# A decoder's feed-forward stage: roundings on Scalar, output rows added by Vector, centring and weighting on GpSimd, down product two batches behind

## What is computed

```python
def rms_norm(x, g):
    var = jnp.mean(x * x, axis=-1, keepdims=True)
    return x * jax.lax.rsqrt(var + EPS) * g
def activation_quant(x):
    scale = 127.0 / jnp.clip(jnp.max(jnp.abs(x), axis=-1, keepdims=True), 1e-05, None)
    return jnp.clip(jnp.round(x * scale), -128, 127) / scale
def bit_linear(x, w, g):
    xn = rms_norm(x, g)
    xq = ste(xn, activation_quant(xn))
    wq = ste(w, weight_quant(w))
    return xq @ wq.T
y = bit_linear(x, gate_w, gate_norm_w)          # 512 -> 2 x 1408
gate, up = jnp.split(y, 2, axis=-1)
h = gate * jax.nn.sigmoid(gate) * up
return bit_linear(h, down_w, down_norm_w)       # 1408 -> 512
# x = x + _L0_ffn_ref(_layernorm(x, axis=-1), ...)
```

## Time and profile before

| | |
|---|---|
| three timed runs | 1201.27, 1203.71, 1204.38 us; median 1203.71 |
| the profiled execution | 1201.6 us, its span 1199.8 us |
| busy share of the span | PE 86%, DVE 68%, ACT 54%, POOL 54% |
| feed-forward stage | from 996.2 us to the end of the span |
| one batch in its loop | 11.42 us |
| mean granted clock of PE over the span | 0.948 |

### The profile page before, as it was taken

One profiled execution on the slowest core, in us unless ns is written; L12 is line 12 of the kernel. 1 busy time (PEld: TensorE's weight loads), 2 busy tenths in 40 slices (PEclk: granted clock), 3 DMA queues, 4 the chain that ended last, 5 costly groups with the idle time before them and its releaser, 6 DMA issues. The chain is left out here.

```text
span 1199.8 us, 25407 instructions
## 1 busy us (share of the span) xinstructions
PE 1026.7 (86%) x9588; PEld 773.0 (64%) x9604; DVE 812.5 (68%) x1487; ACT 652.1 (54%) x1188; POOL 644.6 (54%) x584
## 2 busy tenths in 40 slices
PE   5689999999999999999754899999999944777675
PEld 5568887888888888888542566666666621433332
DVE  7687776666666666667532777778777636888884
ACT  5554555445454544546532476767776522555553
POOL 3663766656565665656635235445453335566663
PEclk9799999999999999999885999999999966899998
DMA  9042634323332332334536687878867010000000
GB/s 346 31 176 106 259 123 161 141 75 137 141 124 89 141 140 74 138 141 170 194 111 142 158 175 174 193 176 187 180 146 157 21 28 24 18 26 17 26 27 27
DMA packets 51135, 147.57 MB, mean 123 GB/s; under 512 B 10448, under 2 KB 24272, under 8 KB 39760
## 3 DMA queue, kind: packets, MB, share of 16 engines
q1 hardware_dynamic: 42288, 86.93, 27.3%
q0 software_dynamic: 8064, 58.72, 13.4%
q10 hardware_dynamic: 672, 0.40, 0.1%
HBM read 120.46 MB, written 25.17 MB: 121 GB/s over the span
## 5 line engine op out<-in xcount | busy, mean ns | idle before, releaser
L1291 DVE TENSOR_REDUCE mx<-Sm 128x4 f32<-128x768 f32 x128 | 122.6, 958 | 83.7 <-PE Sm L1032 81.5
L282 PE MATMUL Qb<-a_xTh,WqH 128*128 128x256 f32 x512 | 147.0, 287 | 3.3 <-DVE a_vl L800 3.2
L283 PE MATMUL Qb<-a_xTl,WqH 128*128 128x256 f32 x512 | 146.3, 286 | 0.0
L284 PE MATMUL Qb<-a_xTh,WqL 128*128 128x256 f32 x512 | 146.1, 285 | 0.0
L627 POOL TENSOR_TENSOR a_pr<-a_pr_plain,a_ph 128x512 fp32r<-128x512 f32 x64 | 83.7, 1308 | 110.9 <-ACT a_ph L447 110.8
L740 DVE TENSOR_TENSOR a_turned<-Qb,sinS 64x512 f32<-64x512 f32 (+1 forms) x144 | 94.9, 659 | 62.5 <-PE Qb L284 45.0
L609 POOL TENSOR_TENSOR a_ql<-a_rot,a_qh 128x512 fp32r<-128x512 f32 x64 | 84.1, 1318 | 98.2 <-ACT a_qh L467 98.0
L1130 ACT ACTIVATE x_ex<-Se 128x768 f32<-128x768 f32 x128 | 103.8, 811 | 60.1 <-PE Se L1032 60.0
L459 ACT ACTIVATE Lb<-Lb 128x512 f32<-128x512 f32 x64 | 37.2, 582 | 171.0 <-PE Ob L354 170.9
L367 PE MATMUL Yb<-a_WoH,a_oH 128*128 128x512 f32 x256 | 104.8, 409 | 4.3 <-POOL a_oN L605 4.3
L282 PEld LDWEIGHTS Qb<-a_xTh,WqH 128*128 128x128 f32 x512 | 99.4, 194 | 7.1 <-issue 2.6
(11 more groups left out here) (202 smaller groups left out, 2840.3 us busy)
## 6 DMA issues: line engine op xcount, KB each, us to landing
a_WoH<-wo_parts POOLq DMA_DIRECT2D x28, 1024.0 KB, 5.2
a_WoL<-wo_parts POOLq DMA_DIRECT2D x28, 1024.0 KB, 7.1
K<-k_parts SPq DMA_DIRECT2D x32, 256.0 KB, 7.7
q_parts<-x_qp SPq DMA_DIRECT2D x16, 384.0 KB, 3.0
k_parts<-x_kp SPq DMA_DIRECT2D x16, 384.0 KB, 3.4
Q<-q_parts SPq DMA_DIRECT2D x16, 384.0 KB, 5.3
a_w_stage<-in_gateT SPq DMA_DIRECT2D x8, 704.0 KB, 4.1
x_w_stage<-in_gateT SPq DMA_DIRECT2D x8, 704.0 KB, 5.2
```

What stands on the lines that cost most here:

```text
L282: pe.matmul(out, w_hi(k), xTh[:, k, :], start=(k == 0), stop=False)
L283: pe.matmul(out, w_hi(k), xTl[:, k, :], start=False, stop=False)
L284: mm = pe.matmul(out, w_lo(k), xTh[:, k, :], start=False, stop=(k == KD - 1))
L1291: dve.tensor_reduce(mx[:, half, at:at + 4].rearrange("p (j a) -> p j a", j=2), Sm[:, :, 0:2 * WIN].rearrange("p j (a c) -> p j a c", a=2), ...
```

## The change

The feed-forward stage is written anew, on the same tiles and chunks:

- The rounding multiplications `xr` and `hr` move from Vector to Scalar (an activation Copy with a scale pointer and MAGIC as bias). Vector keeps `xq` and `hq`.
- `xn` is gone: GpSimd subtracts the row's mean (`xc`) and multiplies by `g1` (`xg`). The row's `scale` is multiplied into `bound` and `ascale` by Vector instead.
- `f1` and `f2` are formed by GpSimd, as two-tensor operations on one column. `f1` has four columns, `hg` two buffers.
- `ys` and GpSimd's add are gone: Vector adds the output rows straight from `Yf`, in one operation `added` that writes `X`.
- The squares are scaled when taken, and the sum of three is formed by `hsum` (of two, early) and `hms`.
- PE's `down` is that of b-2 and stands between gate and up of chunk 0 and chunk 1; the hidden transpose of b-1 stands last in the step. The scale and the rounding of the hidden rows of b-1 come in step b, behind the first `h` of b.
- Every step is written out (b from -3 to 17), with no loop; each small result has a semaphore of its own.

The core of the diff, by queue:

```diff
-            dve.tensor_scalar(t["wf"][:, :], w_mean[:, :], 1.0 / 127.0, None, ALU.mult)
+            for i, factor in ((0, 1.0 / 127.0), (1, 127.0 ** -2)):
+                dve.tensor_scalar(t["wf"][:, i:i + 1], w_mean[:, i:i + 1], factor, None, ALU.mult)
...
+        def steps(step):
+            for b in range(-3, B + 2):
+                step(b)
...
         @block.tensor
             def step(b):
                 if real(b):
-                    pe.wait_ge(xqT_ready, done(b, 1, 0))
-                    for c in range(NC):
-                        gate_up(b, par, c)
+                    gate_up(b, 0)
+                if real(b - 2):
+                    down(b - 2)
+                if real(b):
+                    gate_up(b, 1)
+                if real(b + 1):
+                    rows_turned(b + 1)
+                if real(b):
+                    gate_up(b, 2)
                 if real(b - 1):
+                    hidden_turned(b - 1)
...
         @block.scalar
+            def rows_rounded(b):
+                wait(act, ascale_ready, b + 1)
+                wait(act, xq_ready, b)
+                act.activation(xr[:, :], xg[:, :], ACT.Copy, bias=MAGIC, scale=ascale[:, 0:1]).then_inc(xr_ready, 1)
+            def hidden_rounded(b):
+                wait(act, hscale_ready, b + 1)
+                wait(act, hq_ready, b)
+                act.activation(hr[:, :], hg[b % 2][:, :], ACT.Copy, bias=MAGIC, scale=hscale[:, 0:1]).then_inc(hr_ready, 1)
-                    act.activation(ys[:, :], Yb[:, :], ACT.Copy, scale=f2[:, 1 - par:2 - par]).then_inc(ys_ready, 1)
...
         @block.gpsimd
+                if real(b):
+                    weighted(b, 0)
+                if real(b - 1):
+                    wait(pool, hbound_ready, b)
+                    wait(pool, x_done, b - 2)
+                    pool.tensor_tensor(f2[:, (b - 1) % 2:(b - 1) % 2 + 1], hbound[:, :], t["wf"][:, 1:2], ALU.mult).then_inc(f2_ready, 1)
+                if real(b + 3):
+                    wait(pool, xr_ready, b + 3)
+                    pool.tensor_scalar(xc[:, :], t["X"][:, b + 3, :], t["mv"][:, b + 3, 0:1], None, ALU.subtract).then_inc(xc_ready, 1)
+                    wait(pool, xc_ready, b + 4)
+                    pool.tensor_tensor(xg[:, :], xc[:, :], t["g1"][:, :], ALU.mult).then_inc(xg_ready, 1)
+                if real(b + 2):
+                    wait(pool, bound_ready, b + 3)
+                    wait(pool, h_ready, NC * (b - 1))
+                    pool.tensor_tensor(f1[:, (b + 2) % 4:(b + 2) % 4 + 1], bound[:, :], t["wf"][:, 0:1], ALU.mult).then_inc(f1_ready, 1)
+                if real(b):
+                    weighted(b, 1)
+                    weighted(b, 2)
+                    wait(pool, hms_ready, b + 1)
+                    wait(pool, hscale_ready, b)
                     pool.tensor_tensor(rms[:, :], hms[:, :], t["half"][:, :], ALU.pow).then_inc(rms_ready, 1)
-                    pool.tensor_tensor(x, x, ys[:, :], ALU.add).then_inc(x_done, 1)
...
         @block.vector
+            def added(b):
+                wait(dve, y_full, b + 1)
+                wait(dve, f2_ready, b + 1)
+                dve.scalar_tensor_tensor(out=t["X"][:, b, :], in0=Yb[:, :], scalar=f2[:, b % 2:b % 2 + 1], in1=t["X"][:, b, :],
+                                         op0=ALU.mult, op1=ALU.add).then_inc(x_done, 1)
+            def step(b):
+                if real(b - 1):
+                    hidden_maximum(b - 1, 2)
+                    mean_square(b - 1)
+                if real(b):
+                    hidden(b, 0)
+                if real(b - 1):
+                    hidden_scale(b - 1)
+                if real(b + 2):
+                    rows_scale(b + 2)
+                if real(b - 2):
+                    added(b - 2)
+                if real(b - 1):
+                    hidden_quantised(b - 1)
+                if real(b):
+                    hidden_maximum(b, 0)
+                    hidden(b, 1)
+                if real(b + 2):
+                    rows_quantised(b + 2)
+                if real(b):
+                    hidden_maximum(b, 1)
+                    hidden(b, 2)
+                    first_squares(b)
```

More of the change, by code:

```diff
@@ L1405, in ffn @@
 def ffn(nc, t, out):
-    H0 = 2
     with ExitStack() as ctx:
@@ L1437, in ffn @@
[L1437 to L1440, removed]
+        h, hr = sb("h", [P, F], F32), sb("hr", [P, F], F32)
+        hg = [sb(f"hg{i}", [P, F], F32) for i in range(2)]
+        sq, ss = sb("sq", [P, 512], F32), sb("ss", [P, NC], F32)
+        hq, hqT = sb("hq", [P, F], BF16), sb("hqT", [P, F], BF16)
@@ L1453, in ffn, with wait @@
         block = ctx.enter_context(nc.Block())
[L1455 to L1468, removed]
+        def wait(eng, signal, count):
+            if count > 0:
+                eng.wait_ge(signal, count)
@@ new lines, in down @@
+            def down(b):
+                wait(pe, hqT_ready, b + 1)
+                wait(pe, x_done, b)
+                for k in range(KF):
+                    mm = pe.matmul(Yb[:, :], hqT[:, k * P:(k + 1) * P], t["downQ"][:, k * D:(k + 1) * D],
+                                   start=(k == 0), stop=(k == KF - 1))
+                mm.then_inc(y_full, 1)
+            def step(b):
+                if real(b):
+                    gate_up(b, 0)
[7 more added lines that the diff above has]
+                    gate_up(b, 2)
+                if real(b - 1):
+                    hidden_turned(b - 1)
@@ L1518, in _ @@
+            steps(step)
         @block.scalar
@@ L1531, in squares @@
             def squares(b, c):
                 lo, hi = CHUNKS[c]
[L1533 to L1542 removed]
+                wait(act, h_ready, NC * b + c + 1)
@@ L1595, in _ @@
+            steps(step)
         @block.sync
         def _(sp):
-            with sp.Fori(0, B) as b:
-                sp.wait_ge(x_done, b + 1)
-                sp.dma_start(out[bass.ds(b, 1), :, :].rearrange("a t d -> t (a d)"),
-                             t["X"][:, bass.ds(b, 1), :].rearrange("p a d -> p (a d)")).then_inc(out_done, 16)
-            sp.wait_ge(out_done, 16 * B)
+            for b in range(B):
+                wait(sp, x_done, b + 1)
+                sp.dma_start(out[b], t["X"][:, b, :]).then_inc(out_done, 16)
@@ L1603, in _ @@
+            wait(sp, out_done, 16 * B)
         @block.vector
         def _(dve):
[L1605 to L1615 removed]
```

298 lines of the change are left out of this document (117 added, 181 removed).

## The result

| | median | runs | ratio to before, 95% interval |
|---|---|---|---|
| before | 1202.60 us | 9 | |
| changed | 1207.99 us (1203.02 to 1209.53) | 9 | 1.0036 [1.0019, 1.0052] |

The forecast was 1198.9 with a range up to 1207.5; the median lies 0.5 us above its end and 9.1 above the forecast. The profiled execution of the changed kernel took 1203.0 us, the fastest of its nine; that of before took 1201.6.

A forecast was written before the change was run, and what follows sets the result against it. Vector was taken to be full before, a ring of waits to bound the changed kernel at 11.05 us a batch; +4.1 - 4.1 - 5.6 + 0.8 = -4.8 us gave 1198.9 on the timed runs' scale, range 1193 to 1207.5.

The forecast's parts named there:

- The ring: Feed-forward loop: a closed chain of waits through Vector, Scalar and GpSimd sets the batch period, 11.05 us instead of 11.42.
- (b): Scalar, after the batch's first `h`: `hr`, a square and `xr`, done 4.33 us after that `h` starts.
- step (d): GpSimd: `xq`, asked for during `xg`, takes its turn, then `f1` and `hg` of chunk 1, done at 8.14 us.
- term (c): GpSimd, behind `xr`: `xc` 0.90 us, `xg` 1.27 and two handovers of 0.07, done at 6.63 us.
- Rival 2: GpSimd's `xc` dearer than any two-tensor operation, through its pointer; slower by over 0.3% from 1.55 us; chance 0.12.
- the rule of 1.5 us for each 0.1: Whole kernel: up to 1.1 us, every 0.1 us on `xc` adds 1.5 us to the total.
- The sum's terms: Feed-forward stage: start +4.1, first two batches -4.1, batch 2 to 15 -5.6, end +0.8 us; together -4.8.
- The clock: PE: longest early pause 1.8 us, granted clock 1.0 from about 15 us on, last `down` at the low clock.
- 1 (`xc` at 1.27): GpSimd's new operations cost what its others do: period 11.47 us, total 1205.0, no change that can be told; chance 0.17.
- 3 (no ring, 1181): The chain of waits doesn't close; Scalar's and Vector's chain of some 9.9 us limits a batch, total 1181; chance 0.03.
- 4, on sharing: Vector's `xq` takes its turn ahead of GpSimd's `xg`, up to 0.3 us a batch, +3.9, total 1202.8; chance 0.13.
- `xqT` in the start: Start of the feed-forward stage: Scalar's first `xqT` comes at 9.0 us, behind the second batch's `xr`; before, 4.86.

The follow-up runs named there:

- e1: Changed kernel with GpSimd's `hg` of chunk 1 moved between `xc` and `xg`, ahead of `xg` and `f1`: 1186.98 us, ratio to before 0.9865.
- e2: Changed kernel with the centring `xc` moved from GpSimd to Vector, behind `hq`: 1187.39 us, ratio to before 0.9867.
- e3: Changed kernel without the centring `xc`, so its result is not the same: 1184.36 us, ratio to before 0.9843.
- e4: Changed kernel with the mean given to `xc` as a broadcast second tensor instead of a pointer: 1198.9 us, ratio to before 0.997.
- second profile: The changed kernel, unaltered, timed and profiled once more: 1208.12 us, ratio to before 1.0043; its profiled execution took 1208.1 us.

## Why the prediction was wrong, point by point

**What bounded before, and what the change frees.** Right. `hq` is 0.88 without GpSimd beside it (0.89 forecast), Vector's work fell to 84.2/126 of 11.55, 7.7 us (7.4 forecast), `hr` is 1.47 (1.45) and `xr` 0.71 (0.72). Two sums of work were off without consequence, since neither engine is full: Scalar has 7.3 us a batch (7.9 forecast), PE 9.0 (8.3).

**The ring.** Right in its order, and e1, e2, e3 and e4 each changed the period as the ring has it: 10.20, 10.44, 10.09 and 11.13, where 10.2, 10.5, 10.1 and 11.35 were written with the measured `xc` at hand. Counted from `h` at 1079.31: `xc` starts at 4.33 (forecast for the end of (b): 4.33), the maximum of chunk 1 at 8.69 instead of 8.14, the next `h` at 11.55 instead of 11.05. The whole difference arises between `xc` and that maximum: +0.67 for `xc`, -0.13 as `xq` no longer takes its turn ahead of `f1`. The waits on Vector stand where they were forecast: 1.0 ahead of the maximum of chunk 2, and 2.5 instead of 1.4 ahead of that of chunk 1. Half of this 1.1 is the late maximum (0.55); the other half is a link of step (d) that didn't occur: `xq` was to be held by `xg` and take 1.2, but `xc` was still running when it was asked for, and it took 0.67.

**The step that failed: term (c), `xc` at 0.90.** It is 1.57 in the loop and 1.60 in the mean:

```profile
L1570 POOL TENSOR_TENSOR f_hg<-f_h,g 128x512 f32<-128x512 f32 x32 | 40.7, 1270 | 12.9 <-DVE f_h L1633 11.6
L1581 POOL TENSOR_SCALAR f_xc<-X,mv 128x512 f32<-128x512 f32 x16 | 25.6, 1598 | 31.2 <-ACT f_xr L1532 30.4 <-POOLq L1386 0.8
```

The bounds were 0.52 (a memset) and 1.27 (two tensors), on the argument that the cost grows with the tensors read. But a two-tensor row bounds an operation of another form only if that form adds nothing, and no row showed that. The figure that the prediction cites from the Trainium skill ("GPSIMD Engine Reference", section 3.1), 769 ns for 512 elements, stands there as the best case of a tight loop, and `xc` doesn't come near it; the measured 1.57 decides. Rival 2 is what happened. It had the mechanism and its line, above before from 1.15 on, slower by 0.3% from 1.55 on: its 1205 flat up to 1.45 and 1214 at 2.0 give 1207 at 1.57, measured 1208.0. So near a hit is partly luck: 1207 means 3.3 us more than before, the stage itself took 1.5 more in the first profile and 3.8 in the second, and the other 2.7 of the second lie ahead of the stage. It had a chance of 0.12. An operation form of which the trace has no row, on the ring in 12 of 15 steps, deserved more, and an upper end of `xc` at some 2 us would have put the range's upper end at 1214. e4 tests the rest of the sum: with `xc` at 1.04 the rule of 1.5 us for each 0.1 gives 1201.0; measured 1198.9.

**The sum's terms**, first profile against that of before, forecast in brackets: start +5.45 (+4.1; two `xc` in a row ahead of the first scale are 2 x 0.67 = 1.34 of it, all of the miss). First two batches 21.65 against 24.64, -3.0 (-4.1; forecast 9.5 and 11.05, measured 10.10 and 11.55, one dearer `xc` in each). Batch 2 to 15 146.7 against 146.65, +0.06 (-5.6; eleven periods of 0.5). End 18.93 against 19.81, -0.9 (+0.8, see the clock). Together +1.6, and the profiled times differ by 1.4. The medians differ by 5.4, since the profiled execution was the fastest. The second profile stands for the typical one: start +5.15, batches 0 to 15 -2.85, rest +1.5, and 2.7 ahead of the stage. So of the 9.1 us between forecast and median, the profile's own terms give 6.4, from -4.8 to +1.6, nearly all of it `xc` (the start 1.35, the first two batches 1.1, the loop 5.7, less 1.7 at the end); the others lie in the clock of the last `down` and ahead of the stage.

**The clock.** Expected: 1.0 from 15 us on, the longest pause of the first steps 1.8 us, the last `down` at the low level. The first two didn't hold. PE's longest pause in the first steps is 2.42 us. From batch 1 to 13 it has a pause of 0.8 to 2.2 us in each, and in some batches the gate and up products behind it take 1.87 and 1.68 us instead of 1.03:

```profile
1083.62 0.79 PE L1474 MATMUL T<-ident_b,f_hq 128*128 128x128 bf16 x11 [1.95 <-DVE f_hq L1672]
1085.05 1.87 PE L1466 MATMUL Gb<-gateQ,f_xqT 128*128 128x512 bf16 x4 [0.64 <-DVE f_h L1633]
1086.71 1.68 PE L1466 MATMUL Ub<-gateQ,f_xqT 128*128 128x512 bf16 x4
```

The granted clock of the windows around it:

```profile
1075.00:1080.00 5.00, 4.52 (x22) 1.90 (x21) 2.56 (x7) 2.00 (x4) 2.94 (x5) 1.00 0.00 0
1080.00:1085.00 5.00, 2.45 (x24) 1.50 (x22) 4.79 (x14) 3.81 (x7) 2.82 (x4) 0.96 0.14 52
1085.00:1090.00 5.00, 4.95 (x17) 1.97 (x18) 1.82 (x4) 3.11 (x7) 3.59 (x5) 0.70 0.00 0
```

The level went from 2.4 GHz (granted clock 1.00 until 1084.4) to 1.2 GHz (0.50 from 1085 to 1088) behind a pause, as in the earlier trace rows, where the pause was 4.31. It cost nothing that shows: batches with a mean clock of 0.85 take 11.55 to 11.57 us like those with 1.00. One of the twelve periods from batch 1 on is longer, 11.75, but not by the clock. In the second profile the same batch takes 11.74 with the clock at 1.00, and in both Vector starts `hinv` 0.2 us later:

```profile
1103.69 0.16 DVE L1664 RECIPROCAL f_hinv<-f_hbound 128x1 f32<-128x1 f32 x1 [0.23 <-DVE f_hbound L1661]
```

What delays it there isn't shown. PE isn't on the ring. In the tail it is. There the last `down` was at the low level in the second execution, as forecast (4.88, an end of 21.47 against 20.6), but not in the first (2.55, an end of 18.93).

**The rivals.** 1 (`xc` at 1.27) and 3 (no ring, 1181) fell. 4, on sharing, was small: `xq` is asked for at 1084.8, during `xc`, and takes 0.67, and `xg` starts 0.08 us after `xc` ends and takes 1.31 instead of 1.27. In e4 the turn fell to `f1`, 0.19 more.

**`xqT` in the start** came at 10.4 us, forecast 9; the same two `xc`.

## What to carry to other kernels

When work is taken off the engine that is full, look next for the ring of waits that the new order closes, and lay it out link by link: here the same instructions take 12.2, 11.55, 10.2 or 8.5 us a batch by their order. An operation whose form the trace doesn't hold has no upper bound from another form; if it lies on the ring, give it a chance of its own, or measure it first. And idle time of an engine is room only if what ends it doesn't hang on that engine's own work.
